# Flamingo block with gated cross attention on one core: the sums' turn and product a slot later, one output half in the next unit, weight and context transfers at two fixed places

## The chip, the cores and the metric

One core of a Trainium2 chip. The time is the device time of one execution in microseconds. Before the change it is 2407.74 us, the median of 3 runs (2406.89 to 2412.46). Engines are called by the profile's names: PE (TensorE), DVE (VectorE), ACT (ScalarE), POOL (GpSimd), SP or SyncE (which here only issues transfers).

## The reference, cut to what matters

```python
# x (4, 256, 512), ctx (4, 1601, 512); 32 heads of 128, 8 key/value heads
q = (layernorm(x) @ Wq + bq)                      # per head 256 x 128
k, v = split(ctx @ Wkv + bkv)
scores = einsum("blkgd,bmkd->bkglm", q, k) / sqrt(128)
o = einsum("bkglm,bmkd->blkgd", softmax(scores), v)
x = x + tanh(g_xattn) * (o @ Wo + bo)
x = x + tanh(g_ffn) * ffn(layernorm(x))           # base product and 2 of 8 LoRA experts
```

## The kernel before

The attention is cut into 64 **units**, U = 0 to 63: a batch b = U // 16 and two query heads (512 columns together). A unit has 13 **slots**, one for each tile t of up to 128 of the 1601 context rows. Every engine runs its own program over the same slots, s = 13 U + t, and all meet by semaphores. A slot of PE has always:

- the scores of tile s, three matmuls of 512 columns into `psS` (L414 to L416, each product is made of a high and a low part in fp32r),
- the value product of tile s - 20 (`VAL`), three matmuls into the unit's bank of `psW` (L611 to L613), from `ph` and `pl`,
- and the **jobs** that a table gives for this slot (`AT` and `AT_MEM`, lines 73 to 84, one row for each U % 4, one word for each slot). I call the units by U % 4 kind 0, 1, 2 and 3.

The jobs are: m, the turn of the running maximum of the unit before; s, the turn of the sums of the unit two before (four transposes of `psum_`, L470); r and b, the spreading of reciprocals and maxima over the rows by PE; q, k, v, the next projections; o0 and o1, the two halves of the output product of the unit two before, 6 matmuls of 512 columns each (`proj_o`, through L414 to L416); x, the turn of the next batch's rows.

Around a tile: ACT copies the scores to `xs` (L903), DVE takes the running maximum (`mrun`, L1271), POOL takes the maximum off (`xs`, L832, 17 slots behind), ACT makes the exponential twice, to `psP` (or `pp`, `psum_`) and to `ph` (L993, L996, 18 slots behind), DVE makes `pl` (L1057) and adds to `psum_` (L1302). From unit 16 on, tiles 0 to 2 of a unit are lowered by POOL (L836) and added there (`add_p`, L841), and POOL's `merge` (L847) adds its part to DVE's sums. The merge of one unit stands on POOL in front of the lowering of the next unit's tiles 0, 1 and 2: merge, take-off, lower 0, take-off, lower 1, take-off, lower 2.

For units 16 to 61 the maxima and for units 16 to 60 the sums go through memory (`max_by_mem`, `sum_by_mem`): DVE reduces the turned rows to 128 x 4 numbers, SyncE writes these to `scr_m` or `scr_r` (L690, L701), waits till they have landed, and reads them back as a 128 x 512 tile `mb` or `rbc` (L694, L705). POOL's first take-off of a unit needs `mb`. The sums' way is: s on PE (slot 5), DVE's reduce and reciprocal (L1220, L1222, slot 6), out and back on SyncE (placed at slot 6), DVE's product with `rbc` (L1279, in slot `on_slot`, 9), ACT's `oh` (L1028), DVE's `ol` (L1282, slot 10), o0 on PE (slot 11), o1 (slot 12). DVE works in order, so the product with `rbc` stands in front of the slot's `pl` and sums.

SyncE's program has one queue. Besides the two round trips it loads the weights of the next q, k, v and o (`load`, L673 and L674; 0.5 MB for q and k, 1 MB for v and o, high and low part together), the next batch's context in four pieces (`load_ctx`, L681 and L682, 1.5 MB each), and in units 19 to 26 and 35 to 42 it fetches, and later keeps, two cut pieces of the context of a later batch for each unit (`fetch` L641, `keep_ctx` L663 and L664; POOL cuts at slots 10 and 12, and `kept_at` puts the second keeping four slots later, into the next unit). A load stands in SyncE's program in the slot of the job that frees its place, and waits for that job. In units 18, 34 and 50 the accumulator `acc` is written to memory and the next one loaded (L764 to L770), with a wait for the first between them. SyncE isn't paced by slots, only by its waits.

## Time and profile before

| | |
|---|---|
| median of 3 runs | 2407.74 us |
| the profiled execution | 2417.14 us, its span 2415.2 us |
| busy: PE, weight loads, DVE, ACT, POOL | 2286.6, 1934.7, 1838.8, 1643.8, 1629.7 us |
| DMA packets, bytes | 148798, 282.14 MB |
| granted clock of PE, mean | 0.986 |

Busy time of PE includes matmuls that overlap, so its distance to the span is idle time, but busy time isn't all work. A stretch of the profile is given by its start and end in us from the span's start; I cut units at the first score matmul of their slot 0.

### The profile page before, as it was taken

What the parts mean: (1) busy time and instruction counts of PE and PEld (TensorE: products, weight loads), DVE (VectorE), ACT (ScalarE), POOL (GpSimd) and SP (SyncE); (2) the same over time, 40 slices, a digit from 0 to 9 for tenths busy, and PEclk for the clock granted to TensorE, in tenths of its full rate; (3) what the DMA queues carried; (4) which work ended last, traced back from release to release, by engine and by line L of the source; (5) the groups of instructions that cost most, each with busy time, mean ns of one, the idle gap of its engine ahead of it and who ended that gap; (6) DMA issues with size and microseconds to landing.
All of it is one profiled execution on the core that took longest, in us unless ns stands there. A gap on an engine that the chain in (4) does not pass through costs nothing.

```text
span 2415.2 us, 37259 instructions
## 1 busy us (share of the span) xinstructions
PE 2286.6 (95%) x12205; PEld 1934.7 (80%) x12205; DVE 1838.8 (76%) x3162; ACT 1643.8 (68%) x3117; POOL 1629.7 (67%) x1372
## 2 busy tenths in 40 slices
PE   7999999999999999898999999999899999999888
PEld 6888888888878788787888878788688887878765
DVE  5887988888776777777777767677678778678765
ACT  4776777777676676666777666676667767676653
POOL 5797887877477586675667676765756756656662
PEclk9999999999999999999999999999999999999999
DMA  7344433462234434345243244334433233233301
GB/s 255 128 154 132 133 128 119 155 229 97 100 91 123 119 117 134 92 130 175 62 130 115 83 139 124 114 104 130 146 87 109 85 102 89 65 114 84 92 36 53
DMA packets 148798, 282.14 MB, mean 117 GB/s; under 512 B 27904, under 2 KB 61184, under 8 KB 148352
## 3 DMA queue, kind: packets, MB, share of 16 engines
q1 hardware_dynamic: 148608, 279.77, 36.8%
q8 instruction: 99, 1.62, 0.3%
q14 instruction: 91, 0.75, 0.1%
HBM read 212.66 MB, written 67.05 MB: 116 GB/s over the span
## 4 chain that ended last, share of the span: by engine, by line
PE 76%; DVE 7%; POOL 5%; DMA 5%; issue 3%; ACT 3%; SPq 1%; DVEq 0%; POOLq 0%; ACTq 0%
PE psW L414 12%; PE psW L415 11%; PE psW L416 11%; PE psW L611 6%; PE psS L416 6%; PE psS L414 6%; PE psS L415 6%; PE psW L612 6%; PE psW L613 6%; PE psW L470 3%; DMA scr_r<-rinv 3%; POOL psum_ L847 2%; DVE mrun L1271 2%; DVE psum_ L1302 2%; POOL xs L832 2%
## 5 line engine op out<-in xcount | busy, mean ns | idle before, releaser
L832 POOL TENSOR_TENSOR xs<-xs,mb 128x512 f32<-128x512 f32 (+1 forms) x832 | 1066.3, 1308 | 431.5 <-DMA mb<-scr_m 387.9
L1271 DVE TENSOR_TENSOR mrun<-psS,mrun 128x512 f32<-128x512 f32 (+1 forms) x704 | 484.3, 688 | 416.0 <-ACT xs L903 414.9
L903 ACT ACTIVATE xs<-psS 128x512 f32<-128x512 f32 (+1 forms) x832 | 496.3, 597 | 280.7 <-PE psS L416 270.1
L996 ACT ACTIVATE ph<-xs 128x512 fp32r<-128x512 f32 (+1 forms) x832 | 520.1, 625 | 0.9 <-PE psW L613 0.9
L1057 DVE TENSOR_TENSOR pl<-psP,ph 128x512 fp32r<-128x512 f32 (+1 forms) x672 | 458.2, 682 | 27.9 <-ACT ph L996 25.0
L1302 DVE TENSOR_TENSOR psum_<-psP,psum_ 128x512 f32<-128x512 f32 (+1 forms) x672 | 456.2, 679 | 0.0
L993 ACT ACTIVATE psP<-xs 128x512 f32<-128x512 f32 (+1 forms) x672 | 402.1, 598 | 1.7 <-DVE psum_ L1302 1.6
L611 PE MATMUL psW<-ph,vh 128*128 128x512 f32 (+1 forms) x832 | 341.0, 410 | 44.2 <-DVE pl L1057 30.8
L414 PE MATMUL psS<-ql,kh 128*128 128x512 f32 (+1 forms) x832 | 339.2, 408 | 7.0 <-DVE mrun L1271 5.7
L612 PE MATMUL psW<-pl,vh 128*128 128x512 f32 (+1 forms) x832 | 330.1, 397 | 0.0
L613 PE MATMUL psW<-ph,vl 128*128 128x512 f32 (+1 forms) x832 | 330.1, 397 | 0.0
L415 PE MATMUL psS<-qh,kh 128*128 128x512 f32 (+1 forms) x832 | 329.4, 396 | 0.0
L416 PE MATMUL psS<-qh,kl 128*128 128x512 f32 (+1 forms) x832 | 329.3, 396 | 0.0
L611 PEld LDWEIGHTS psW<-ph,vh 128*128 128x128 f32 (+1 forms) x832 | 157.7, 189 | 109.2 <-DVE pl L1057 39.7
L414 PE MATMUL psW<-wvl,ch 128*128 128x256 f32 (+1 forms) x832 | 240.2, 289 | 4.4 <-DVE vl L1057 4.4
L415 PE MATMUL psW<-wvh,ch 128*128 128x256 f32 (+1 forms) x832 | 235.1, 283 | 0.0
L416 PE MATMUL psW<-wvh,cl 128*128 128x256 f32 (+1 forms) x832 | 234.5, 282 | 0.0
L613 PEld LDWEIGHTS psW<-ph,vl 128*128 128x128 f32 (+1 forms) x832 | 157.7, 190 | 38.3
L908 ACT ACTIVATE kh<-psW,bkv_sb 128x384 fp32r<-128x384 f32 (+1 forms) x128 | 76.4, 597 | 163.1 <-PE psW L416 163.1
L612 PEld LDWEIGHTS psW<-pl,vh 128*128 128x128 f32 (+1 forms) x832 | 158.5, 190 | 34.6 <-issue 1.7
L416 PEld LDWEIGHTS psS<-qh,kl 128*128 128x128 f32 (+1 forms) x832 | 153.9, 185 | 39.6 <-issue 1.0
L414 PE MATMUL psW<-cl,wkh 128*128 128x384 f32 (+1 forms) x512 | 177.7, 347 | 5.4 <-DVE cl L1057 5.4
(185 smaller groups left out, 4454.5 us busy)
## 6 DMA issues: line engine op xcount, KB each, us to landing
wqh<-scr_wq SPq DMA_DIRECT2D x96, 256.0 KB, 3.9
wql<-scr_wq SPq DMA_DIRECT2D x96, 256.0 KB, 4.4
woh<-scr_wo SPq DMA_DIRECT2D x48, 512.0 KB, 5.1
wol<-scr_wo SPq DMA_DIRECT2D x48, 512.0 KB, 6.9
mb<-scr_m SPq DMA_DIRECT2D x46, 256.0 KB, 4.2
rbc<-scr_r SPq DMA_DIRECT2D x45, 256.0 KB, 3.7
scr_wq<-wqh SPq DMA_DIRECT2D x32, 256.0 KB, 2.0
scr_wq<-wql SPq DMA_DIRECT2D x32, 256.0 KB, 2.5
```

The source lines that it names most:

```text
L414: eng.matmul(o, lh, rl, start=first, stop=False)
L415: eng.matmul(o, lh, rh, start=False, stop=False)
L416: return eng.matmul(o, ll, rh, start=False, stop=last)
L611: eng.matmul(o, vh[0:rows, t, hs], hi, start=t == 0, stop=False)
L612: eng.matmul(o, vh[0:rows, t, hs], lo, start=False, stop=False)
L613: eng.matmul(o, vl[0:rows, t, hs], hi, start=False, stop=t == NT - 1).then_inc(s_pv)
L832: eng.tensor_tensor(tile, tile, mb[0:rows_of(t), U % 2, :], ALU.subtract).then_inc(s_sub)
L903: return eng.activation(hi, src, ACT.Copy)
L996: eng.activation(ph[0:rows, T % RP, :], xs[0:rows, T % RX, :], ACT.Exp).then_inc(s_h)
L1057: return eng.tensor_tensor(lo, src, f32(hi), ALU.subtract)
L1271: eng.tensor_tensor(run, psS[0:rows, s % 2, :], a, ALU.max).then_inc(s_m)
L1302: eng.tensor_tensor(total, p, total, ALU.add).then_inc(s_a)
```

## The change

What it does, in units 18 to 61 (`quiet`, the units whose sums went through memory before, less the last):

- the sums' turn s stands in slot 6, the product with `rbc` in slot 10, `oh` in 10, `ol` in 11, o0 in slot 12, and o1 in slot 0 of the next unit, behind m. The other jobs are moved around them: in kind 0 there are v0 to v4 in slots 7 to 11, in kind 1 v7 is in slot 5 and slot 10 is empty, in kind 2 q0 and k3 stand a slot later and v11, v12 in slots 2 and 3; POOL's steps stay.
- SyncE places the sums' round trip at slot 7, and the transfers that stood beside the jobs at slot 3 (first q half, o) and slot 9 (second q half, k, v). The context pieces are loaded at slot 9 of a batch's unit 13, slots 3 and 9 of unit 14 and slot 3 of unit 15.
- POOL's second context cut of a unit stands in slot 11, and both pieces are kept a slot behind their cut, in the same unit.
- the accumulator's way out and in stands at slot 3 of units 18, 34, 50, behind the loads of that slot, and DVE's statistics at slot 2.
- the sums of unit 60 go through PE (`MEM_SUM` is one less), so unit 62 has the old table's job r and its o0 in slot 10.

```diff
-    MEM_LO, MEM_MAX, MEM_SUM = 16, UN - 2, UN - 3
+    MEM_LO, MEM_MAX, MEM_SUM = 16, UN - 2, UN - 4
...
+    def quiet(U):
+        return U >= 2 and sum_by_mem(U - 2)
...
     def on_slot(V):
-        return 9 if sum_by_mem(V) else 8
+        return 10 if sum_by_mem(V) else 8
...
     AT_MEM = [
-        "m q0 b k3 q1 s - v0 v1 v2 v3 o0 o1",
-        "m,v4 v5 b,q0 v6 k0 s,v7 q1 k1 v8 v9 v10 o0 o1",
-        "m,v11 k2 b,v12 q0 k3 s - - q1 - - o0,x0 o1,x1",
-        "m q0 b k0 q1 s k1 - - k2 - o0 o1",
+        "m q0 b k3 q1 - s v0 v1 v2 v3 v4 o0",
+        "m v5 b,q0 v6 k0 v7 s,q1 k1 v8 v9 - v10 o0",
+        "m k2 b,v11 v12 q0 k3 s - q1 - - x0 o0,x1",
+        "m q0 b k0 q1 - s,k1 - - k2 - - o0",
     ]
...
+        if U >= 3 and sum_by_mem(U - 3):
+            jobs[NT * U].append(("o", U - 3, 1))
...
-        cuts[NT * (NU * b + 3 + i // 2) + (10, 12)[i % 2]].append(("c", n, 0))
+        cuts[NT * (NU * b + 3 + i // 2) + (10, 11)[i % 2]].append(("c", n, 0))
...
-                if t == 6 and sum_by_mem(U - 2):
+                if t == 7 and quiet(U):
                     sum_to_lanes(U - 2)
...
-                for kind, n, part in jobs[s]:
+                for kind, n, part in [] if quiet(U) else jobs[s]:
...
+                if quiet(U) and t == 3 and 2 * U + 4 < 2 * UN:
+                    load("q", 2 * U + 4, 2 * NU, s_q, 2 * U + 3)
+                if t == 3 and U >= 3 and sum_by_mem(U - 3):
+                    load("o", U - 2, NU, s_o, 2 * U - 4)
+                if quiet(U) and t == 9:
+                    if 2 * U + 5 < 2 * UN:
+                        load("q", 2 * U + 5, 2 * NU, s_q, 2 * U + 4)
+                    if U % 2 == 0 and U // 2 + 1 < NK:
+                        load("k", U // 2 + 1, 8, s_k, 2 * U + 4)
+                    if U % 4 == 2 and U // 4 + 1 < 4 * B:
+                        load("v", U // 4 + 1, 4, s_v, NT * (U // 4) + NT)
+                if quiet(U) and b + 1 < B and (u, t) in ((13, 9), (14, 3), (14, 9), (15, 3)):
+                    load_ctx(b + 1, ((13, 9), (14, 3), (14, 9), (15, 3)).index((u, t)))
...
-                if u == 2 and t == 1 and 1 <= b < B:
+                if u == 2 and t == 3 and 1 <= b < B:
                     sp.wait_ge(s_acd, 32 * b)
```

PE in unit 44 (kind 0), from the value product of slot 5 on. `psum_` is the sums' tile, `psS` the scores of the next slot. Before:

```order
L611 MATMUL psW<-ph,vh 128x512
L612 MATMUL psW<-pl,vh 128x512
L613 MATMUL psW<-ph,vl 128x512
L470 MATMUL psW<-ident,psum_ 128x128 x4
L414 MATMUL psS<-ql,kh 128x512
L415 MATMUL psS<-qh,kh 128x512
L416 MATMUL psS<-qh,kl 128x512
L611 MATMUL psW<-ph,vh 128x512
L612 MATMUL psW<-pl,vh 128x512
L613 MATMUL psW<-ph,vl 128x512
L414 MATMUL psS<-ql,kh 128x512
```

and with the change:

```order
L614 MATMUL psW<-ph,vh 128x512
L615 MATMUL psW<-pl,vh 128x512
L616 MATMUL psW<-ph,vl 128x512
L417 MATMUL psS<-ql,kh 128x512
L418 MATMUL psS<-qh,kh 128x512
L419 MATMUL psS<-qh,kl 128x512
L614 MATMUL psW<-ph,vh 128x512
L615 MATMUL psW<-pl,vh 128x512
L616 MATMUL psW<-ph,vl 128x512
L473 MATMUL psW<-ident,psum_ 128x128 x4
L417 MATMUL psS<-ql,kh 128x512
```

The turn of the sums stands one whole slot (six matmuls) further on, with nothing put in front of it in this kind.

SyncE in unit 22, from behind the maxima's way back up to the reciprocals' way out (`scr_c` and `stg` are the context pieces, `wv`, `wq`, `wo`, `wk` the weights, h and l their high and low parts). Before:

```order
L673 DMA wvh<-scr_wv 128x1024
L674 DMA wvl<-scr_wv 128x1024
L663 DMA scr_c<-cst 128x384
L664 DMA scr_c<-stg 128x384
L641 DMA stg<-in_ctxT 128x384
L673 DMA wqh<-scr_wq 128x512
L674 DMA wql<-scr_wq 128x512
L673 DMA woh<-scr_wo 128x1024
L674 DMA wol<-scr_wo 128x1024
L673 DMA wkh<-scr_wk 128x512
L674 DMA wkl<-scr_wk 128x512
L701 DMA scr_r<-rinv 128x4
```

and with the change:

```order
L644 DMA stg<-in_ctxT 128x384
L676 DMA wqh<-scr_wq 128x512
L677 DMA wql<-scr_wq 128x512
L676 DMA woh<-scr_wo 128x1024
L677 DMA wol<-scr_wo 128x1024
L704 DMA scr_r<-rinv 128x4
```

Four weight transfers are left in front of the reciprocals where there were eight, and the keeping of a context piece is gone from here.

SyncE in the same unit, from behind the reciprocals' way back to the maxima of the unit after (`scr_m`). Before:

```order
L673 DMA wqh<-scr_wq 128x512
L674 DMA wql<-scr_wq 128x512
L663 DMA scr_c<-cst 128x384
L664 DMA scr_c<-stg 128x384
L641 DMA stg<-in_ctxT 128x384
L690 DMA scr_m<-nm 128x4
```

and with the change:

```order
L676 DMA wqh<-scr_wq 128x512
L677 DMA wql<-scr_wq 128x512
L676 DMA wkh<-scr_wk 128x512
L677 DMA wkl<-scr_wk 128x512
L676 DMA wvh<-scr_wv 128x1024
L677 DMA wvl<-scr_wv 128x1024
L666 DMA scr_c<-cst 128x384
L667 DMA scr_c<-stg 128x384
L666 DMA scr_c<-cst 128x384
L667 DMA scr_c<-stg 128x384
L644 DMA stg<-in_ctxT 128x384
L693 DMA scr_m<-nm 128x4
```

The weights of k and v and both context pieces now stand here, in front of the maxima.

## Rows read from the trace of the kernel before

**Rows 1.** The page: the chain that ended last, by line; transfers, median us to landing.
```profile
PE psW L414 12%; PE psW L415 11%; PE psW L416 11%; PE psW L611 6%; PE psS L416 6%; PE psS L414 6%; PE psS L415 6%; PE psW L612 6%; PE psW L613 6%; PE psW L470 3%; DMA scr_r<-rinv 3%; POOL psum_ L847 2%; DVE mrun L1271 2%; DVE psum_ L1302 2%; POOL xs L832 2%
...
rbc<-scr_r SPq DMA_DIRECT2D x45, 256.0 KB, 3.7
```

**Rows 2.** PE's groups by form: busy us, mean ns, idle before, releasers.
```profile
L611 PE MATMUL psW<-ph,vh 128*128 128x512 f32 x768 | 315.1, 410 | 44.2 <-DVE pl L1057 30.8 <-POOL pl L836 13.4
...
L414 PE MATMUL psW<-wol,oh 128*128 128x512 f32 x256 | 106.6, 416 | 16.9 <-issue 15.3 <-POOL wkh L820 1.1 <-DVE ol L1282 0.5
...
L470 PE MATMUL psW<-ident,psum_ 128*128 128x128 f32 x256 | 45.7, 301 | 30.0 <-POOL psum_ L847 28.3 <-DVE psum_ L1307 1.7
```

**Rows 3.** Stretches of one unit each: 44, 45, 50, 43, 57, 62; us, then busy us of PE, PEld, DVE, ACT, POOL, clock, DMA share, GB/s.
```profile
1603.81:1637.89 34.08, 33.06 (x184) 28.36 (x182) 27.21 (x47) 24.64 (x47) 23.45 (x19) 1.00 0.34 94
1637.89:1677.25 39.36, 39.13 (x232) 34.68 (x230) 28.67 (x51) 26.55 (x51) 22.98 (x19) 1.00 0.46 148
1827.21:1862.08 34.87, 32.95 (x171) 27.32 (x170) 28.45 (x50) 24.46 (x46) 21.15 (x17) 1.00 0.47 151
1570.34:1603.81 33.47, 31.78 (x160) 26.70 (x158) 25.48 (x44) 23.99 (x45) 21.98 (x18) 1.00 0.32 93
2071.51:2114.61 43.10, 40.67 (x232) 36.18 (x230) 29.27 (x57) 28.87 (x54) 22.91 (x19) 0.96 0.22 62
2256.44:2301.12 44.68, 37.46 (x175) 30.25 (x174) 35.25 (x49) 25.05 (x47) 22.12 (x17) 0.89 0.35 106
```

**Rows 4.** The same for units 22, 36 and 46.
```profile
791.25:832.75 41.50, 35.70 (x171) 29.17 (x170) 27.82 (x48) 24.45 (x46) 26.66 (x23) 0.92 0.43 131
1305.04:1340.97 35.93, 33.39 (x183) 28.21 (x182) 26.99 (x47) 24.63 (x47) 28.18 (x25) 1.00 0.43 125
1677.25:1720.17 42.92, 35.41 (x180) 28.93 (x178) 27.62 (x48) 25.04 (x47) 26.76 (x20) 0.92 0.55 190
```

**Rows 5.** Timeline of unit 44, slots 4 to 7: start, us, engine, idle before.
```profile
1613.23 2.56 POOL L832 TENSOR_TENSOR xs<-xs,mb 128x512 f32<-128x512 f32 x2 [8.62 <-DMA mb<-scr_m]
...
1617.80 1.27 POOL L847 TENSOR_TENSOR psum_<-pp,psum_ 128x512 f32<-128x512 f32 x1 [2.01 <-DVE psum_ L1302]
...
1619.13 0.75 PE L470 MATMUL psW<-ident,psum_ 128*128 128x128 f32 x4 [1.02 <-POOL psum_ L847]
...
1620.27 1.30 POOL L836 TENSOR_TENSOR pl<-psum_,ph 128x512 fp32r<-128x512 f32 x1
...
1621.80 0.40 PE L611 MATMUL psW<-ph,vh 128*128 128x512 f32 x1
```

**Rows 6.** Timeline of unit 22, slots 6 to 11, SyncE's queue, DVE and PE.
```profile
811.13 1.49 SPq L701 DMA_DIRECT2D scr_r<-rinv  x1
...
818.18 0.32 SPq L705 DMA_DIRECT2D rbc<-scr_r  x1
...
822.19 0.70 DVE L1279 TENSOR_TENSOR psW<-psW,rbc 128x512 f32<-128x512 f32 x1 [3.78 <-DMA rbc<-scr_r]
...
823.92 0.50 PE L611 MATMUL psW<-ph,vh 128*128 128x512 f32 x1 [4.08 <-DVE pl L1057]
```

**Rows 7.** Instructions and transfers of scr_r: the 45 ways out of the reciprocals.
```profile
DMA to landing us min/median/max: 1.4/3.4/9.6
```

**Rows 8.** SyncE's timeline, unit 34: the accumulator out and in.
```profile
1241.19 0.42 SPq L764 DMA_DIRECT2D scr_x<-acc  x1
1246.12 0.32 SPq L767 DMA_DIRECT2D acc<-scr_b  x1
```

**Rows 9.** Timeline of unit 62, slots 9 to 11.
```profile
2281.50 7.80 DVE L1131 TENSOR_SCALAR hn<-x,mv,rstd 128x512 f32<-128x512 f32 x1
...
2284.08 4.93 POOL L832 TENSOR_TENSOR xs<-xs,mb 128x512 f32<-128x512 f32 x4
...
2290.05 0.76 PE L414 MATMUL psS<-ql,kh 128*128 128x512 f32 x1 [5.73 <-DVE mrun L1271]
```

**Rows 10.** Timeline of unit 57, slot 5: the turn of the sums.
```profile
2090.72 0.85 PE L470 MATMUL psW<-ident,psum_ 128*128 128x128 f32 x4 [2.43 <-POOL psum_ L847]
```

More of the change, by code:

```diff
@@ L86, in gated_block @@
         names_of = {0: "k1 - k2 v0 q0 k3 q1 v1 - v2 - v3 -", UN: "- - - - - s - r - - o0 - o1",
-                    UN + 1: "- - - - - s - r - - o0 o1"}.get(U, (AT_MEM if U >= 2 and sum_by_mem(U - 2) else AT)[U % 4])
+                    UN + 1: "- - - - - s - r - - o0 o1"}.get(U, (AT_MEM if quiet(U) else AT)[U % 4])
         for t, names in enumerate(names_of.split()):
@@ L134, in gated_block @@
         b, i = divmod(n, 16)
-        cuts[NT * (NU * b + 3 + i // 2) + (10, 12)[i % 2]].append(("c", n, 0))
+        cuts[NT * (NU * b + 3 + i // 2) + (10, 11)[i % 2]].append(("c", n, 0))
     cut_at = [(p, 0) for p in first] + [(p, s) for s in range(SLOTS) for p in cuts[s]]
     order = [p for p, s in cut_at]
-    def kept_at(z):
-        return z + 4 if z > NT * NU and z % NT == 12 else z + 1
     fetches = {s: [] for s in range(SLOTS)}
@@ L152, in gated_block @@
         if no >= len(first) + 2:
-            s = max(s, at - 10, kept_at(cut_at[last][1]))
+            s = max(s, at - 10, cut_at[last][1] + 1)
             assert s <= at, (p, at, s)
@@ L734, in _ @@
                     max_to_lanes(U - 1)
-                if t == 6 and sum_by_mem(U - 2):
+                if t == 7 and quiet(U):
                     sum_to_lanes(U - 2)
-                for kind, n, part in [p for z in (s - 4, s - 1) if kept_at(z) == s for p in cuts.get(z, [])]:
+                for kind, n, part in cuts.get(s - 1, []):
                     if kind == "c":
@@ L754, in _ @@
                         load_ctx(n // 8 + 1, part)
-                if t == 3 and sum_by_mem(U - 3):
-                    load("o", U - 2, NU, s_o, 2 * (U - 3) + 2)
-                if u == 14 and t == 1 and b + 1 < B:
+                if quiet(U) and t == 3 and 2 * U + 4 < 2 * UN:
[11 more added lines that the diff above has]
+                    load_ctx(b + 1, ((13, 9), (14, 3), (14, 9), (15, 3)).index((u, t)))
+                if (u, t) == ((13, 11) if b else (14, 1)) and b + 1 < B:
                     sp.wait_ge(s_xt, 2 * b + 2)
@@ L1324, in _ @@
                     dve.wait_ge(s_stat, 1)
-                if u == 2 and t == 0 and 1 <= b < B:
+                if u == 2 and t == 2 and 1 <= b < B:
                     for i in range(2):
```

## The prediction

> **What bounds the kernel now.** I read the page's chain first: it runs through PE's matmuls, and its largest piece that isn't compute is the way of the reciprocals to memory, 3% of the span [rows 1]. PE is busy for 2286.6 of 2415.2 us, so all its gaps together are 129 us. Next come PE's groups by form, for what ends the gaps [rows 2]: value products wait 44.2 us, 30.8 of it for `pl` by DVE and 13.4 for `pl` by POOL; the turn of the sums waits 30.0 us, 28.3 of it for POOL's merge; o0 waits 16.9 us. These three are 91 us, and the change touches each.
>
> Then the units themselves. An ordinary unit of kind 0, 1, 2, 3 takes 34.08, 39.36, 34.87 and 33.47 us [rows 3]. Some take more: 22 and 46, both kind 2, take 41.50 and 42.92, and 36, kind 0, takes 35.93 [rows 4]. Six units of kind 2 are like the first two (22, 26, 30, 38, 42, 46), three of kind 0 like the third (20, 36, 40). Units 57 and 62 stand out for reasons of their own, 43.10 and 44.68 us [rows 3].
>
> The timeline of unit 22 shows why: the reciprocals' way out is issued at 811.13, but the way back only at 818.18, 7.05 us later, since it waits for the 2 KB to land. DVE waits 3.78 us at the product with `rbc` and, working in order, reaches `pl` late; PE stands 4.08 us at the value product behind it [rows 6]. In front of these 2 KB SyncE has just issued the eight weight transfers, after a context piece had held it up. Over all 45 the way out takes 1.4 us at the least, 3.4 as median and 9.6 at most [rows 7], the last in a unit where a piece of the next batch's context stands in front.
>
> **The change, part by part.**
>
> *Late reciprocals.* Unit 22 is 6.6 us over an ordinary kind 2, 46 is 8.1 over. I take 6.6 for each of six, 39.6 us; for the three of kind 0, whose worst is 1.85 over, 1.5 each, 4.5 us. With the change the k and v weights and the kept pieces stand behind the round trip, so this goes: **44.1 us**. Two things stay in front.
>
> In units 30 and 46, q, o and a context piece (3 MB) are issued when q0 ends in slot 4. I count from there. A slot is six matmuls of 512 columns; in unit 44 nine of these and the four transposes take 2.67 us [rows 5], so 0.235 each, 1.4 us for a slot, 0.5 for a turn, and a k3 about 2.4. The turn ends at 3.8 + 1.9 = 5.7 us, the reciprocals are ready at 6.7, and DVE comes to the product in slot 10 at about 13.3 (slots 7 to 9 with q1, 5.6, then scores, copy and maximum of slot 10, 2.0). The longest way out landed after 9.6 us [rows 7], with such a piece issued just before it; here the piece has 4 us of start, so I take 4 to 8 us. The way back takes 3.7 [rows 1]: `rbc` is there at 14.4 to 18.4, 1 to 5 us late. As a third of the bytes that stood there are gone, I take 1.5 for each: **-3.0 us**.
>
> In units 18, 34 and 50 the accumulator's way out stands behind q and o, and SyncE waits for it: 4.93 us when it had only `mb` in front of it [rows 8]. Issued at 2 us and landed at 7 to 10, it holds the reciprocals' way out by 0 to 3 us, of which a margin of 1 to 2 us is free. I take 1 each: **-3.0 us**.
>
> The Trainium skill (DMA: Bandwidth & Descriptors, Queues, rings and completion order) says that a transfer's semaphore increment lands only after every earlier write of the same DMA engine. By it position in SyncE's program decides, as rows 6 and 7 also look, and it speaks against the change in these five units alone, where large transfers are moved ahead of the small one.
>
> *The slots.* The turn's cover is one slot. But POOL's chain behind the merge isn't moved. In unit 44 [rows 5] POOL's merge runs 1617.80 to 1619.07, the turn waits for it, POOL's lowering of tile 0 runs 1620.27 to 1621.57, and PE takes tile 0's value product at 1621.80. With the change PE does slot 6 first, comes to the turn at about 1619.4 without a wait, and is at the value product of slot 7 at 1620.6, where it now waits till 1621.6. So **kind 0** gains 0.2 us, not the 1.2 that the turn's wait seems to give: the lowering is late next. **Kind 1** has v7 and q1 there as well, 2.8 us more of cover; its share of the turn's wait goes, 0.7. **Kind 2** has k3 (2.4 us) in front of the turn, so its waits for the turn (0.3) and for POOL's lowering (1.1; with kind 3 these are the 13.4 us of rows 2) go. Its o0 wait stays: DVE has product, lowering and sums of two slots to do while PE has empty slots, before and after. Less a bit for DVE's queue, 1.0. **Kind 3** keeps slots 7 and 8 empty, so POOL's lowering of tile 2 stays late, and the product in slot 10 no longer has k2 (2.1 us) beside it: its o0 wait grows by about a microsecond, which eats the 0.5 to 0.7 gained before. I take -0.3. The sum is 1.6 us in four units; units 18 to 61 are eleven of each kind: **17.6 us**. The ends: nothing or -5 if DVE's queue is worse, and 40 if half of all idle time in the four (7.8 us) goes.
>
> o1 in slot 0 adds 1.4 us of PE work there and takes it from slot 12: nothing. It gives POOL's chain more room: in unit 44 the first take-offs wait for `mb` till 1613.23, end at 1615.79, and POOL then is idle 2.01 us till the merge can start [rows 5]. With o1 this margin becomes 3.4.
>
> *Unit 57* is 3.7 us over its kind [rows 3]. ACT's detour for the statistics makes the merge late, and the turn waits 2.43 us for it [rows 10]. With v7 and a slot of scores and values, 2.8 us, in front, all of it goes: **3.0 us** beside the 0.7 counted above; bounds 0 and 3.0.
>
> *Unit 62* is 9.8 us over its kind. It loses the round trip. But DVE's normalisation `hn` takes 7.80 us here and PE waits 5.73 us for the maximum behind it [rows 9]; `rbc` is not what it waits for, and `hn` stays where it is. I take only a share of what follows it, as `ol` is one slot earlier: **2.5 us**; bounds 0 and 9.8.
>
> The Trainium skill (SBUF — State Buffer, Who interferes with whom) states that DVE in a two-port mode and GpSimd exclude each other for whole instructions. The timeline agrees: `hn` ends 2289.30, just behind POOL's row of take-offs, 2289.01 [rows 9]. If instead the round trip were the cause, this term would be 9.8 and the sum 7 us more.
>
> *The rest.* The spread of unit 60's reciprocals by PE is 0.5 us, once. Loads at slot 9 have over half a unit till their use: nothing.
>
> **Sum.** 44.1 - 3.0 - 3.0 + 17.6 + 3.0 + 2.5 - 0.5 = 60.7 us. The profiled execution took 2417.1, so it would show 2356.4; it lies 9.4 over the median of the runs, which stands for 2407.7 - 60.7 = **2347 us**.
>
> **The rivals.**
>
> *The slots bring nothing or cost.* If the waits only move, from the turn to POOL's lowering and from slot 11 to slot 12, in all four kinds, the slots' term is -5 to 5, and the five crowded units may stand at their upper ends (another 10 us off): 2365 to 2382. For it speaks kind 0, where I count just this; against it that kinds 1 and 2 have work to put there. Chance 0.22.
>
> *The slots bring all.* If o0's waits go too, which would need DVE's queue to be shorter than I read it, the term is 40 and unit 62 may give more: 2307 to 2327. Against it is that slots 9 to 11 are empty in kind 2. Chance 0.12.
>
> *The maxima become late instead.* Context pieces and k and v weights now stand before the maxima's way out, which `mb` and POOL's first take-off wait for. The margin is 2.0 + 1.4 us in kinds 0 and 3 and more in the others. If the way out took 7 us, as the reciprocals' did [rows 6], `mb` would be 5.6 later; 22 units at 2.2 us and nothing in the others are 48 us, and with POOL's whole chain late in all 44 units by over 2 us it is past the gain: 2347 + 88 = 2435, slower. It decides from a delay of 3.4 us, and is slower than before from about 5 us in kinds 0 and 3 and the other two hit as well. Against it: these loads are issued a third of a unit before the maxima, and only 16 units have context pieces. Chance 0.04.
>
> *The change doesn't reach the reciprocals:* SyncE comes to its slot 7 no sooner than before, as q0's load is still waited for in kind 2. Then only the slots count, 2385 to 2400. But q0 ends 6 us before they are ready. Chance 0.04.
>
> **How the numbers follow.** My forecast's own case, 2330 to 2364, has 0.58. With the two next to it the range 2322 to 2382 leaves out about 2 in 10. A measurement of this kernel can tell 0.3% (7 us) from no change: faster 0.94, within it 0.02, slower 0.04.
>
> **What would show it.** In the profile after: the waits for `rbc` by DVE's product near zero but in units 18, 30, 34, 46, 50; unit 22 at 34 us; the turn's wait for POOL under 3 us in all, with a wait of the value product for POOL's lowering that grows from 13.4 to 20 us or more; o0 waiting longer in kind 3; unit 57 near 39 us; unit 62 above 41. Wrong would be: kind 0 shorter by over a microsecond, take-offs waiting for `mb` until the merge is due, or unit 62 at 35 us.

## The result and the profile after

| | before | after |
|---|---|---|
| median of 4 runs each | 2408.64 us (2406.89 to 2412.46) | 2389.33 us (2385.76 to 2395.64) |
| the profiled execution, its span | 2417.14, 2415.2 us | 2395.64, 2393.7 us |
| granted clock of PE, mean | 0.986 | 0.988 |

After to before is 0.9921, with a 95% interval of 0.9896 to 0.9945: some 19 us faster, where 61 were forecast. The direction is right, and the time lies above the range. One execution among all runs, the profiled one of the first run below, took 4477.52 us; it counts in the median of that run alone, and the kernel was run once more for its trace.

PE's groups by form, after: busy us, mean ns, idle before, releasers; to be read beside [rows 2].

```profile
L614 PE MATMUL psW<-ph,vh 128*128 128x512 f32 x768 | 317.6, 413 | 48.0 <-DVE pl L1072 25.9 <-POOL pl L851 21.6
...
L417 PE MATMUL psW<-wol,oh 128*128 128x512 f32 x256 | 110.6, 432 | 31.3 <-issue 29.7 <-POOL wkh L835 1.1 <-DVE ol L1297 0.5
...
L473 PE MATMUL psW<-ident,psum_ 128*128 128x128 f32 x256 | 40.2, 279 | 3.3 <-DVE psum_ L1322 1.7 <-POOL psum_ L862 1.6
```

The turn's wait is gone, 30.0 to 3.3 us, and the other two have grown: the value products wait 8.2 us more for POOL's `pl`, though 4.9 less for DVE's, and o0 waits 14.4 us more. The three were 91.1 us and are 82.6. Not all of the o0 row's growth is the slots': unit 62 has 5.6 us of the 14.4, since its wait of 5.73 us stood at the scores before [rows 9] and stands at o0 now, 6.33 us (the line is shown further down). Units of kind 3 have 6.1 us of it and those of kind 2 have 2.7.

Units of the changed kernel, in this order 44, 45, 54, 43 (ordinary, kinds 0 to 3), then 22, 30, 34, 50, 57 and 62; columns as in [rows 3].

```profile
1581.85:1617.41 35.56, 34.49 (x195) 29.90 (x194) 27.67 (x49) 25.05 (x48) 23.63 (x19) 1.00 0.27 90
1617.41:1655.08 37.67, 37.67 (x220) 33.34 (x219) 27.59 (x48) 26.07 (x50) 22.85 (x19) 1.00 0.40 126
1952.35:1986.82 34.47, 32.91 (x172) 27.43 (x170) 27.12 (x47) 24.45 (x46) 20.43 (x17) 1.00 0.41 123
1547.71:1581.85 34.14, 32.03 (x159) 26.63 (x158) 26.36 (x45) 24.07 (x45) 28.50 (x24) 1.00 0.32 96
790.18:824.65 34.47, 32.91 (x172) 27.42 (x171) 27.10 (x47) 24.44 (x46) 23.00 (x19) 1.00 0.49 150
1073.88:1113.30 39.42, 35.80 (x180) 29.74 (x178) 29.17 (x51) 24.93 (x47) 25.39 (x19) 0.93 0.53 166
1221.21:1262.75 41.54, 34.98 (x171) 28.71 (x170) 29.75 (x53) 24.44 (x46) 22.52 (x18) 0.90 0.47 132
1803.98:1844.98 41.00, 34.82 (x172) 28.58 (x171) 29.57 (x53) 24.45 (x46) 22.53 (x18) 0.92 0.43 128
2056.51:2094.28 37.77, 37.77 (x219) 33.14 (x218) 28.10 (x54) 28.49 (x53) 22.22 (x18) 1.00 0.22 71
2236.11:2279.23 43.12, 36.63 (x185) 30.26 (x184) 35.37 (x51) 25.22 (x48) 21.24 (x17) 0.92 0.33 104
```

Three readings come straight from these lengths.

- Unit 22 is an ordinary unit now, and so are 26, 38 and 42, and 20, 36 and 40: of the 29.1 us that these seven were over their kind, 28.6 are gone.
- The four kinds take 34.08 + 39.36 + 34.87 + 33.47 = 141.78 us before [rows 3] and 35.56 + 37.67 + 34.47 + 34.14 = 141.84 after. A v (1.4 us) went from kind 1 to kind 0; beyond that nothing was gained in four units.
- Units 34 and 50, ordinary before (50 was 34.87 [rows 3]), take 41.54 and 41.00. Unit 30 takes 39.42 and unit 46 40.22. The four are 24.3 us over their kind, and the units behind them (31, 35, 47) another 2.6. In units 30 and 46 some 0.8 us each is no wait but the turns of the next batch's rows, which the others of their kind don't have (an estimate from the kernel before: unit 14, which has them, takes 34.79 us and unit 10, which hasn't, 34.02).

The timelines of unit 34 show the third: SyncE's queue from the first load of slot 3 on, with the end of DVE's reciprocals between, then DVE's and PE's late instruction.

```profile
1236.63 0.32 SPq L676 DMA_DIRECT2D wqh<-scr_wq  x1
...
1238.41 0.43 SPq L779 DMA_DIRECT2D scr_x<-acc  x1
...
1243.72 0.18 DVE L1237 RECIPROCAL rinv<-ssum 128x4 f32<-128x4 f32 x1
...
1247.37 0.32 SPq L782 DMA_DIRECT2D acc<-scr_b  x1
1247.79 0.38 SPq L704 DMA_DIRECT2D scr_r<-rinv  x1
1251.61 0.32 SPq L708 DMA_DIRECT2D rbc<-scr_r  x1
...
1256.66 0.70 DVE L1294 TENSOR_TENSOR psW<-psW,rbc 128x512 f32<-128x512 f32 x1 [5.46 <-DMA rbc<-scr_r]
...
1258.00 0.79 PE L614 MATMUL psW<-ph,vh 128*128 128x512 f32 x1 [5.78 <-DVE pl L1072]
```

SyncE stands 8.96 us between the accumulator's way out and its way in, and the reciprocals' way out is behind both: ready at 1243.90, it is issued 3.9 us later. It then takes 3.82 us, and DVE's product starts when the way back has landed, 5.05 after its issue. This is the same row of waits as in unit 22 before [rows 6], with other bytes in front. The way out is slow here (1.44 us in the ordinary unit 54), the way back isn't: its median over the kernel is

```profile
rbc<-scr_r SPq DMA_DIRECT2D x44, 256.0 KB, 4.5
```

where it was 3.7 [rows 1], and in unit 54 it takes 5.3, so that DVE's product there starts only 0.2 us after it has landed. SyncE issues 2 MB of weights 1.3 us behind it (slot 9); whether they slow it no run separates. Behind PE's 5.78 us of standing, the rest of the slot runs at another clock; the window from there to the unit's end (its seventh number is the granted clock) is

```profile
1258.00:1262.75 4.75, 4.34 (x9) 3.00 (x10) 4.70 (x8) 3.12 (x7) 0.11 (x1) 0.50 0.74 292
```

0.50 is 1.2 GHz, where it had been 1.00, 2.4 GHz, ahead of the wait. PE is busy for 34.98 us in unit 34 and for 32.91 in its like, unit 54, so the fallen clock adds some 2 us to the wait.

The second reading first in kind 0. POOL and PE of unit 44, to be read beside [rows 5]:

```profile
1597.24 1.30 POOL L862 TENSOR_TENSOR psum_<-pp,psum_ 128x512 f32<-128x512 f32 x1 [3.35 <-DVE psum_ L1317]
1598.49 1.31 POOL L847 TENSOR_TENSOR xs<-xs,mb 128x512 f32<-128x512 f32 x1
...
1598.78 0.63 PE L473 MATMUL psW<-ident,psum_ 128*128 128x128 f32 x4
...
1599.75 1.28 POOL L851 TENSOR_TENSOR pl<-psum_,ph 128x512 fp32r<-128x512 f32 x1
...
1601.18 0.47 PE L614 MATMUL psW<-ph,vh 128*128 128x512 f32 x1 [1.07 <-POOL pl L851]
```

The turn doesn't wait, as forecast, and the value product two steps on waits for the lowering, as forecast. POOL is idle for 3.35 us ahead of the merge (3.4 forecast), and only then, behind the merge, makes the take-off that stands in front of the lowering.

In kinds 2 and 3 the o0 wait is the one to look at. Before, in units 50 and 43:

```profile
1857.88 0.47 PE L414 MATMUL psW<-wol,oh 128*128 128x512 f32 x1 [0.94 <-issue]
1599.61 0.47 PE L414 MATMUL psW<-wol,oh 128*128 128x512 f32 x1 [0.39 <-issue]
```

and after, in units 54, 43 and 62:

```profile
1985.37 0.47 PE L417 MATMUL psW<-wol,oh 128*128 128x512 f32 x1 [1.08 <-issue]
1580.40 0.47 PE L417 MATMUL psW<-wol,oh 128*128 128x512 f32 x1 [0.94 <-issue]
2271.76 0.76 PE L417 MATMUL psW<-wol,oh 128*128 128x512 f32 x1 [6.33 <-issue]
```

Kind 2 had this wait before as well; it is kind 3 where it grew, by 0.55 us. What else the four kinds gained and gave back per unit: kind 0 lost its turn's wait of 1.02 us and got 1.07 at the lowering; kind 1 lost 0.23 at the turn; kind 2 lost 0.80 at the lowering and got 0.26 at the scores, for DVE's maximum, and 0.14 at o0; kind 3 lost 0.98 at the turn and got 0.50 more at the lowering, 0.34 for DVE's `pl` and the 0.55 at o0.

### The profile page after: what moved, and what is told of

It reads as the page before. It is cut to its first block, busy times and chain, and to the rows that moved or that the text cites. A ratio compares the mean times of both kernels' runs of the same rounds, so it can differ in the third digit from the quotient of the medians.

```text
span 2393.7 us, 37301 instructions
## 1 busy us (share of the span) xinstructions
PE 2281.9 (95%) x12209; PEld 1935.1 (81%) x12209; DVE 1838.1 (77%) x3162; ACT 1643.9 (69%) x3118; POOL 1627.5 (68%) x1372
## 4 chain that ended last, share of the span: by engine, by line
PE 76%; POOL 9%; DVE 6%; issue 3%; DMA 3%; ACT 2%; SPq 0%; POOLq 0%; ACTq 0%; DVEq 0%
PE psW L417 12%; PE psW L418 11%; PE psW L419 11%; PE psW L614 7%; PE psW L616 6%; PE psS L419 6%; PE psW L615 6%; PE psS L417 6%; PE psS L418 6%; POOL xs L847 4%; POOL pl L851 3%; PE psW L473 2%; DVE pl L1072 2%; POOL psum_ L862 1%; ACT xs L918 1%
## 5 line engine op out<-in xcount | busy, mean ns | idle before, releaser
L862 POOL TENSOR_TENSOR psum_<-pp,psum_ 128x512 f32<-128x512 f32 x47 | 60.9, 1295 | 191.5 <-DVE psum_ L1317 191.5
```

## The experiments

Each is the changed kernel with the edit shown; times are medians, and all ratios are to the kernel before, run on the same chip. The kernel before gave 2410.55, 2410.68 and 2413.76 us in the three sets. The changed kernel ran only beside the 2408.64 us above, so a distance to it or from one set to another carries 2 to 5 us of which chip it was.

**The accumulator ahead of the o load.**

```diff
-                if u == 2 and t == 3 and 1 <= b < B:
+                if u == 2 and t == 2 and 1 <= b < B:
                     sp.wait_ge(s_acd, 32 * b)
```

> The changed kernel, with the accumulator's way out and in placed at slot 2 of units 18, 34 and 50, before the loads of slot 3, instead of behind them. Nothing else differs. Theory A (transfers that the change left in front of the reciprocals' way out hold it up, through SyncE's wait for the accumulator): units 34 and 50, which took 41.54 and 41.00 us in the changed kernel, fall to 34.5 like the other units of kind 2, and the time falls by 12 to 14 us, to about 2376. Theory B (the wait is in DVE's statistics or the accumulator's sum itself, not in the queue): both units stay at 41 us and the time at 2389.

> The kernel of e1_acc_early once more, for its trace. By theory A of that run (the o load ahead of the accumulator's way out and in is what made it late) the accumulator is out and in before the trip of the reciprocals: units 34 and 50 within 1.5 us of their kind (34.5 us) instead of 41.5 and 41.0, acc in at least 3 us earlier against the unit's start; the rest of the kernel unchanged, one time of 2374 to 2380 us.

Measured: 2377.65 us, 0.9866 [0.9846, 0.9887], 11.7 below the changed kernel (2376.86 us without the execution of 4477.52 us); one more, for the trace, took 2379.01. That is in the 2374 to 2380 of theory A. In that trace unit 50 takes 34.80 us, and unit 34 is this:

```profile
1218.58:1253.31 34.73, 33.06 (x171) 27.43 (x170) 28.41 (x51) 24.44 (x46) 20.37 (x17) 1.00 0.49 158
```

and SyncE's queue in unit 34, with DVE's last statistics between:

```profile
1224.74 0.32 SPq L779 DMA_DIRECT2D scr_x<-acc  x1
...
1230.15 0.69 DVE L1116 BATCH_NORM_STATS2 steps<-acc 128x6 f32<-128x512 f32 x1
...
1230.92 0.32 SPq L782 DMA_DIRECT2D acc<-scr_b  x1
1233.99 0.32 SPq L676 DMA_DIRECT2D wqh<-scr_wq  x1
...
1241.29 0.32 SPq L704 DMA_DIRECT2D scr_r<-rinv  x1
1242.73 0.32 SPq L708 DMA_DIRECT2D rbc<-scr_r  x1
```

The accumulator is on its way 6.2 us after the unit's start instead of 17.2, since SyncE doesn't stand at the q load's wait for the job of slot 4 first. The way in is still issued 6.18 us after the way out, but that is no longer the transfer: the way out has landed after 3.8 us (8.9 in the changed kernel), and the way in also waits for DVE's statistics of `acc`, whose sums end at 1230.84. It is on its way before q and o are issued, and the reciprocals are out 1.44 us after their issue. One slot in SyncE's program is 13 us in the two units, and theory A holds with its size.

**Context pieces apart from the round trip.**

```diff
-                if quiet(U) and b + 1 < B and (u, t) in ((13, 9), (14, 3), (14, 9), (15, 3)):
-                    load_ctx(b + 1, ((13, 9), (14, 3), (14, 9), (15, 3)).index((u, t)))
+                for c in {(13, 9): (0, 1), (14, 9): (2,), (15, 3): (3,)}.get((u, t), ()):
+                    if quiet(U) and b + 1 < B:
+                        load_ctx(b + 1, c)
```

> The changed kernel, with the second context piece loaded together with the first, at slot 9 of a batch's unit 13, instead of at slot 3 of unit 14. Theory A (bytes in front of the 2 KB decide): unit 30 falls from 39.42 to 34.5 and unit 46 from 40.22 to 34.5, the units behind them (31 and 47, 34.68 and 35.46) stay 0.5 to 1.3 over their kind, since the third piece still stands in front of the maxima; together -10 to -11 us, to about 2379. Theory B (the 3 MB only move: now the maxima of unit 29, which stand behind q and two pieces, come late, and POOL with them): unit 30 keeps 2 us or more, as a wait of POOL for mb beyond the merge, and the gain is under 6 us.

Measured: 2387.26 us, 0.9909 [0.9892, 0.9926], 2 below the changed kernel. Units 30 and 46 came down to 37.61 and 37.63, not to 34.5. With the piece gone from in front of the trip, PE's turn of the next batch's second x tile (`cst`) was late in both, by 2.6 us, behind DVE's `xtl` of the first. The time is as theory B had it, but its reason is not: no product waits for `rbc` in these two units any more, and PE's wait is not POOL's for `mb`. Nor could they come to 34.5, since their x turns alone are some 0.8 us. My first explanation was that the x loads, at slot 11 of units 29 and 45 (the change moved them there from slot 1 of units 30 and 46, which the list of what it does leaves out), stood behind 3 MB of context. Two later runs, with the x loads ahead of the context and with POOL's normalizations elsewhere, test it.

**POOL's take-off ahead of its merge.**

```diff
-                "S0,S1 M,S2 L0,S3 L1,S4 L2,S5 A2,S6 S7 S8 S9 S10 S11 S12 -",
+                "S0,S1,S2 M L0,S3 L1,S4 L2,S5 A2,S6 S7 S8 S9 S10 S11 S12 -",
```

> The changed kernel, with POOL's take-off of tile 2 in front of its merge instead of behind it; the order of all else stays. Theory A (what holds PE in kinds 0 and 3 is POOL's chain behind the merge: merge, take-off, lower 0, take-off, lower 1, take-off, lower 2): POOL is idle 3.35 us in front of the merge, so the take-off costs nothing there, and the lowering comes 1.3 us sooner. Kind 0 loses its wait at slot 7 (1.40 us), kind 3 0.5 to 1.1 at slot 9, kind 2 nothing: -20 to -25 us, to about 2367. Theory B (the wait would only move on, to o0 at slot 12 behind DVE's queue): kind 0, with v0 to v4 in front of o0, still gains, kind 3 nothing: -10 to -15 us. Theory C (ACT's exponential of tile 0 is late, not POOL): no change, 2389.

Measured: 2376.13 us, 0.986 [0.9842, 0.9878], 13 below. Units 44 and 43 of its trace:

```profile
1571.20:1605.63 34.43, 34.43 (x196) 29.91 (x194) 27.66 (x49) 25.04 (x48) 23.75 (x19) 1.00 0.33 93
1537.78:1571.20 33.42, 31.84 (x159) 26.71 (x158) 26.39 (x45) 23.98 (x45) 28.66 (x24) 1.00 0.29 94
```

Kind 0 is 1.13 us shorter and kind 3 0.72, so eleven of each would be 20 us. Some of it is given back: in kind 3 units of the stretches with context cuts (unit 39 takes 34.91) the turn in slot 6 waits again for POOL. The time is in theory B's range, while kind 3 does gain, as theory A had it.

**The old slots.** Before's table of jobs, product at slot 9, round trip at slot 6; transfers, cuts and the rest as changed.

```diff
-        return 10 if sum_by_mem(V) else 8
+        return 9 if sum_by_mem(V) else 8
...
-                if t == 7 and quiet(U):
+                if t == 6 and quiet(U):
```

> The changed kernel with the slots of before: the job table with the turn in slot 5, the product in slot 9, o0 and o1 in slots 11 and 12 of one unit, the round trip at slot 6. SyncE's two places, the context pieces, the accumulator at slot 3 and unit 62 through PE stay. Theory A (the slots bring nothing but in unit 57): as the changed kernel plus the 3.6 us of unit 57, so 2391 to 2395; kinds 0 to 3 at 34.08, 39.36, 34.9 and 33.5 us as before the change, and the turn waits for POOL again. The forecast's theory (the slots bring 17.6 us besides): 2410. In kind 2 there is now less time between slot 3's transfers and the reciprocals' way out than with the new slots by nothing (q0 is a slot earlier as well), so units 30, 34, 46, 50 stay long.

Measured: 2396.67 us, 0.994 [0.9917, 0.9964], 7.3 over the changed kernel, with intervals of the ratios that overlap; 1.7 above theory A's range and 13 below what the forecast's 17.6 us would make. Units 44, 45, 54, 43 and 57:

```profile
1583.94:1618.03 34.09, 33.06 (x184) 28.38 (x183) 27.18 (x47) 24.67 (x47) 23.40 (x19) 1.00 0.34 94
1618.03:1657.41 39.38, 39.14 (x232) 34.68 (x231) 28.67 (x51) 26.59 (x51) 22.93 (x19) 1.00 0.41 121
1953.41:1988.31 34.90, 32.96 (x171) 27.31 (x170) 26.88 (x46) 24.47 (x46) 21.15 (x17) 1.00 0.40 121
1550.43:1583.94 33.51, 31.83 (x159) 26.72 (x158) 26.03 (x45) 23.90 (x45) 28.81 (x24) 1.00 0.32 93
2055.90:2099.28 43.38, 40.69 (x232) 36.08 (x230) 29.28 (x57) 28.89 (x54) 22.74 (x19) 0.96 0.22 61
```

The first four are 141.88 us, before's lengths one by one and the changed kernel's sum: the slots alone bring nothing in ordinary units. Units 22, 26, 38 and 42 are at 34.90 to 34.93 here and 20, 36 and 40 at 34.09, so the late reciprocals went by the transfers' places and not by the slots. Unit 57 is long again, 4.0 us over its kind. That is about what the slots brought: the two profiled executions have spans of 2396.3 and 2393.7 us; the rest of the 7.3 between the medians is within the spread.

**`ol` a slot earlier,** behind `pl` and the running sum of the product's own slot.

```diff
-                if 0 <= V < UN and t == on_slot(V) + 1:
-                    dve.wait_ge(s_oh, V + 1)
-                    eng.scalar_tensor_tensor(ol[:, :], bank_of(("pv", V, 0)), ...
...
+                if 0 <= V < UN and t == on_slot(V):
+                    dve.wait_ge(s_oh, V + 1)
+                    eng.scalar_tensor_tensor(ol[:, :], bank_of(("pv", V, 0)), ...
```

> The changed kernel, with one DVE instruction elsewhere: ol, the lower part of the turned output, is formed at the end of slot 10 behind pl and the running sum, instead of in slot 11 behind the running maximum. In the changed kernel's trace o0 in slot 12 waits for it in units with U % 4 = 2 and 3 (issue 1.08 us in unit 54, 0.94 us in unit 43), where slot 12 loses 1.8 us; the kinds 0 and 1 have an empty slot or little wait there. Theory A (what the slots saved at the turn came back as this wait): some 0.9 us off in two of four units, 11 groups of four, so 15 to 20 us, 2369 to 2375 us beside 2389. Theory B (the wait only hands on to the running maximum and the next scores, since DVE stands at ol until ACT has oh): within 4 us of the changed kernel, with slot 12 shorter and slot 11 or the next slot 0 longer by as much.

Measured: 2368.76 us, 0.9819 [0.9803, 0.9834], 20.6 below the changed kernel. The output product's wait in its groups by form:

```profile
L417 PE MATMUL psW<-wol,oh 128*128 128x512 f32 x256 | 107.9, 422 | 7.4 <-issue 7.4
```

It falls from 31.3 to 7.4 us, of which 8.2 are unit 62's and come back there as a wait of 6.25 us at the scores. Ordinary units of kinds 2 and 3 take 33.71 and 33.56 instead of 34.47 and 34.14, and kind 1 37.47 instead of 37.66. The gain has theory A's size, a little over. But it isn't only what the slots had moved: kind 2, which gains most, waited 0.94 us for o0 in the kernel before too. No run has this edit with the old slots, so how much of the 20.6 us needs the new ones isn't shown. In the changed kernel the wait is DVE's queue: in unit 54 the product, `pl`, the sums and the maximum of slot 11 follow each other without a gap, and `ol` comes last.

```profile
1981.98 0.69 DVE L1294 TENSOR_TENSOR psW<-psW,rbc 128x512 f32<-128x512 f32 x1
1982.58 0.68 DVE L1072 TENSOR_TENSOR pl<-psP,ph 128x512 fp32r<-128x512 f32 x1
1983.18 0.68 DVE L1317 TENSOR_TENSOR psum_<-psP,psum_ 128x512 f32<-128x512 f32 x1
1983.91 0.69 DVE L1286 TENSOR_TENSOR mrun<-psS,mrun 128x512 f32<-128x512 f32 x1
1984.52 0.74 DVE L1297 SCALAR_TENSOR_TENSOR ol<-psW,bkv_sb,oh 128x512 fp32r<-128x512 f32 x1
```

PE's o0 starts at 1985.37, 0.11 behind the end of `ol`. The profile puts PE's 1.08 us down to "issue"; the run shows that it was `ol`.

**Three edits together.** The accumulator at slot 2, the take-off first, the context pieces apart, each as above, and the x loads ahead of the context:

```diff
-                if (u, t) == ((13, 11) if b else (14, 1)) and b + 1 < B:
+                if (u, t) == ((13, 8) if b else (14, 1)) and b + 1 < B:
```

> The changed kernel with three edits: accumulator out and in at slot 2 of its unit, GpSimd's take-off of slot 2 ahead of the merge, context pieces 0 and 1 at slot 9 of unit 13, 2 and 3 at slots 9 and 3 of the next two units, and the next x loads at slot 8 of unit 13, ahead of the context. Theory A (the losses lie in different units, so the gains add): 12 for the accumulator, 13 for the take-off, 2 for the pieces and 2 x 4.5 for the x loads that stood behind the context in that experiment, together 36, so 2350 to 2358 us, and units 30 and 46 within 1 us of their kind (34.5), units 34 and 50 within 3. Theory B (the pieces only choose which transfer is late): units 30 and 46 keep over 2 us, 2360 to 2366.

Measured: 2357.58 us, 0.9776 [0.9761, 0.9791]. One by one the three had brought 27 us, together they bring 31.8: the gains add, and nothing shows where the rest comes from. Units 34 and 50 are at 34.45 and 34.58. But units 30 and 46 still take 37.61 and 37.63, exactly what they took with the x loads behind the context. So the x loads' place was not it, and my explanation falls, though the time is at the edge of theory A's range.

**The same with `ol` in slot 10,** by the edit shown above.

> The three edits together and ol at the end of slot 10. Theory A: what ol brings alone comes off here too, since it lies in another slot (12) of the units than the take-off's (7 and 9): e6_three_together minus e5's gain, 2336 to 2342 if e5 gives 15 to 20. Theory B: nothing beyond e6_three_together.

Measured: 2341.11 us, 0.9709 [0.9691, 0.9727], 16.5 below the last. The two edits meet no common limit. Unit 30 is at 37.63 once more; POOL there, while PE is in slots 9 to 12, makes two normalizations between its take-offs:

```profile
1084.37 2.07 POOL L902 TENSOR_SCALAR xraw<-xraw,mv,rstds 128x512 f32<-128x512 f32 x1
1086.43 2.07 POOL L902 TENSOR_SCALAR cst<-cst,mv,rstds 128x512 f32<-128x512 f32 x1
```

**The old slots with the take-off first,** the two edits above together.

> The kernel with the old slots of jobs (before's table, product at slot 9, turn of the sums at slots 4 and 5, reciprocals' trip at slot 6), the rest as changed (2396.7 us when it ran), and with GpSimd's take-off of slot 2 ahead of the merge. It tells whether the 13 us of the take-off are the new slots' gain set free or GpSimd's order alone. Theory A (the new slots leave the turn time for the merge, and only so can the take-off go first): with the turn in slot 5 again, the merge 1 us later makes it wait 1 us longer, and units come out as without the edit or longer, 2395 to 2408 us. Theory B (GpSimd's order was the only limit): 2380 to 2386 us.

Measured: 2398.45 us, 0.9947 [0.9932, 0.9962], the old slots' time within the spread. PE's turn of the sums in it:

```profile
L470 PE MATMUL psW<-ident,psum_ 128*128 128x128 f32 x256 | 45.8, 303 | 37.2 <-POOL psum_ L859 35.4 <-DVE psum_ L1319 1.7
```

The turn waits 37.2 us here, 32.9 with the old slots alone, 30.0 in the kernel before [rows 2]. Theory A has the time, but its reason only in part: in an ordinary unit of kind 0 the turn waits 1.02 us as before and not a microsecond more, because the take-off fits into POOL's idle time and PE waits for the merge, which comes no sooner. Units 23, 27 and 39 are 8.7 us longer together than with the old slots alone. (Unit 62 happens to be 8.8 us shorter, of which more at the end; without that the edit would have cost.) The same edit brings 13 us with the new slots and nothing or less with the old ones: only where PE no longer waits for the merge does it matter what stands behind the merge. The new slots' worth is thus room that POOL's order did not use.

**GpSimd's normalizations of x at another place.** The kernel of the three edits and `ol`, with

```diff
-                if u == 14 and t == 8 and b + 1 < B:
+                if u == 14 and t == (3 if b else 8) and b + 1 < B:
                     pool.wait_ge(s_stat, 1)
```

> The kernel of e7_together_ol with GpSimd's two normalizations of the next x tiles (x_norm, 2.07 us each, one behind the other) at slot 3 of units 30 and 46, where GpSimd waits for its maxima, instead of slot 8. In e7_together_ol units 30 and 46 lose 4.74 and 4.77 us in slot 12, their kind elsewhere 1.08. Theory A (not a transfer but GpSimd: the 4.1 us of the two stand ahead of its add and of the take-offs, so ACT's exponentials, DVE's queue and the bank of the first x turn are late): 3.7 off in each of the two units, 7.4 in all, 2332 to 2336 beside 2341. Theory B (PE's turn waits for the x tiles' transfer or for its bank whatever GpSimd does): within 2 us of 2341.

Measured: 2340.37 us, 0.9694 [0.9669, 0.9718]; by the medians nothing. In the trace units 30 and 46 fell to 35.88 and 35.86, 1.8 us each, half of what A expected. The median doesn't resolve 3.5 us here: five runs lie between 2333.70 and 2343.22, and other units (27 with 36.90 for 34.01) were longer in this trace.

**The context as changed.** The last kernel, with the pieces and the x loads where the change has them.

> e9_x_norm_early with the context pieces and the x loads where the changed kernel has them (pieces at slot 9 of unit 13, 3 and 9 of 14, 3 of 15; x loads at slot 11 of unit 13, for units 29 and 45). It tells how much of the 5 us that units 30 and 46 lost beyond their kind in the changed kernel is transfers ahead of the reciprocals' trip and how much GpSimd's normalizations. Theory A (mostly GpSimd): within 3 us of e9. Theory B (mostly the piece at slot 3, 1.5 MB ahead of the trip at slot 7): units 30 and 46 lose 3 to 5 us each in slot 12, 6 to 10 us beyond e9.

Measured: 2345.22 us, 0.9719 [0.9694, 0.9743], 4.9 over the last. Units 30 and 46 take 39.29 and 38.93, 6.5 us more together, at the lower end of theory B, whose 6 to 10 us of time the median doesn't reach. So with the normalizations out of the way the transfers ahead of the trip cost 3.4 and 3.1 us in these units, and with the transfers out of the way the normalizations cost 1.8. The two waits hide each other: moving the transfers alone had given 1.8 and 2.6 us in the changed kernel, and unit 30 with only the normalizations moved (39.29) is hardly shorter than with neither (39.45 in the run of `ol` alone). With both moved, units 30 and 46 are still 2.1 us over the 33.8 of their kind, of which some 0.8 is the x turns; PE waits 1.4 us for DVE's `xtl` at the second of them. What makes that late is open.

**`hn` on GpSimd.** The kernel of the normalizations' run, with the first `hn` of unit 62 on the other engine.

```diff
-                if s in (TN - 14, TN - 11):
-                    i = 2 if s == TN - 14 else 4
+                if s in (TN - 17, TN - 14, TN - 11):
+                    i = {TN - 17: 0, TN - 14: 2, TN - 11: 4}[s]
...
-                for i in {TN - 18: (0,), TN - 17: (1,), ...
+                for i in {TN - 17: (1,), ...
```

> e9_x_norm_early with the first ffn normalization of unit 62 (hn, TENSOR_SCALAR, 5.99 us on DVE in e7_together_ol, 7.24 in the changed kernel, 1.05 in e8_old_slots_takeoff) moved from DVE to GpSimd, at slot 9 behind its add. Theory A (on DVE it waits until GpSimd's unbroken run of work ends, 2270.1 in the changed kernel's trace, and does not work for that long; on GpSimd it costs its own 2.07 us): slot 10 of unit 62 loses 2 us instead of 4.5 and slot 11 under 1 instead of 1.5, together 3 to 4 us off, 2328 to 2333. Theory B (GpSimd's take-offs are what unit 62 waits for, hn only stands beside them): no gain, or up to 2 us more.

Measured: 2331.67 us, 0.9662 [0.9639, 0.9685], 8.7 below it. Unit 62 takes 35.72 us, after 42.11; GpSimd's `hn` takes 2.07 us there, and this is the unit:

```profile
2181.95:2217.67 35.72, 35.20 (x185) 29.21 (x184) 28.33 (x49) 25.48 (x48) 20.59 (x16) 1.00 0.41 126
```

Theory A holds, and in the unit's length with nearly twice its size. This is the fastest of the kernels: 3.4% below the kernel before, and 58 us below the changed kernel.

## Why the prediction was right and wrong

*What bounds the kernel* was read rightly: the reciprocals' trip, the turn, the value products and o0 are what the runs could move. POOL's normalizations of x it does not have.

*Late reciprocals, 44.1 us.* In the seven units where nothing large stands in front, 28.6 us went for the 30.9 of the forecast; over all nine the units were 44.4 over their kind. The rule of the Trainium skill that the prediction weighed (DMA: Bandwidth & Descriptors, Queues, rings and completion order) agrees with the traces of this case: 7.05 us for 2 KB behind transfers [rows 6], 1.44 us in unit 34 once the accumulator is ahead. Of the five units that it pointed at, four were late.

*The crowded units, 6.0 us: this term failed first, they cost 26.9.* For unit 34 I took the accumulator's way out to land 7 to 10 us after the loads' issue; it did at 10.7. The reciprocals were ready 7.3 us after it (6.7 by my count), so they were held 3.9 us and not "0 to 3". And I let their way out behind it run at its undisturbed 1.4 us; it took 3.8, issued right behind 0.5 MB of `acc` coming in. These two add in a row, 6.3 us. Against them stood no "margin of 1 to 2 us": I had taken 3.7 us for the way back, and in this kernel it takes up to 5.3 with nothing in front, which leaves 0.2 us to spare in unit 54. Unit 34's took 5.0, 0.3 less, and DVE came to the product about half a microsecond after `rbc` would have been there; that leaves the 5.46 us which the row shows. With the fallen clock it makes 7.1 and 6.5 us in units 34 and 50 against "1 each". Unit 18, with no o load in front, takes 33.34 us; it has 1.4 us less to do than its kind (no o1 of an earlier unit), so it lost about 0.3. For units 30 and 46 the forecast of `rbc` "1 to 5 us late" was right, DVE waited 2.9 and 3.7 us. Then I took 1.5 "as a third of the bytes that stood there are gone", which no row said: the lateness went to PE whole, as 3.2 and 4.0 us at the value product, and the clock in the 5.4 us behind it was 0.50 in unit 30. That POOL's two normalizations of x would be the next wait once the transfers are away I had not seen at all.

*The slots, 17.6 us: the second term that failed, they gave nothing.* This was the first rival, chance 0.22, and its 2365 to 2382 was still too low, since it left the crowded units at 16 us. By kinds: in kind 0 I had +0.2, it was -0.1 (1.48 longer, with a v of 1.4 moved in). Kind 1 had +0.7, was +0.3. Kind 2 had +1.0, was +0.4. Kind 3 had -0.3, was -0.7. Part of it I had read wrongly off the kernel before: a unit of kind 1 waits 0.23 us for the turn and not 0.7, one of kind 2 doesn't wait for the turn at all (I had 0.3), and for the lowering 0.80 and not 1.1. That is 1.1 us in four units that weren't there to be gained. "Its o0 wait stays" was right for kind 2, 0.94 and 1.08 us. Kind 3's o0 wait grew by 0.55, for which I had "about a microsecond". What I left out is what comes back elsewhere: 0.26 us at the scores in kind 2 ("less a bit for DVE's queue"), 0.34 at DVE's `pl` and 0.50 more at POOL's lowering in kind 3, and in kind 0 the lowering took all of the turn's wait and not all but 0.2 us. The upper end of 40 had no ground either: all idle time of PE in the four units is 4.9 us by [rows 3], 141.78 less 136.92 busy, so that half of it is 27 us in eleven groups and not 40.

*Unit 57, 3.0:* measured 3.74 over its kind before, 0.10 after, so 3.6. *Unit 62, 2.5:* 1.6, although it took in 1.4 us of work that I hadn't counted, o1 of unit 59. That `hn` and not `rbc` is what it waits for was right, and the last run shows it: the wait went with `hn`, to a unit of 35.72 us. The second rule that was weighed (SBUF — State Buffer, Who interferes with whom) agrees with this trace as with the one before, where `hn` on DVE ends with POOL's row of work; one other run, at the end, has it otherwise. The rows are these, DVE and POOL of unit 62 of the changed kernel:

```profile
2263.16 7.24 DVE L1146 TENSOR_SCALAR hn<-x,mv,rstd 128x512 f32<-128x512 f32 x1
...
2265.20 4.92 POOL L847 TENSOR_TENSOR xs<-xs,mb 128x512 f32<-128x512 f32 x4
```

POOL ends at 2270.12, `hn` at 2270.40.

**The sum again,** with what was measured in the profiled executions: 44.4 - 26.9 - 0.7 (eleven groups of four) + 3.6 + 1.6 is 22.0 us; unit 18 is 1.2 shorter beyond what its kind is, the units before it and the last stretch together 1.8 longer. That gives 21.4, and the two profiled executions are 21.5 us apart, the medians 19.3. Against the 60.7 of the forecast, the crowded units are 21 us short and the slots 18.

The maxima were never late (POOL is idle 3.35 us ahead of its merge), and SyncE came to the trip in time but in units 34 and 50, so the two small rivals were rightly small.

## What to carry to other kernels

A wait that goes away by shifting a chain is worth only what the next instruction of the same chain doesn't take back. Follow every engine's queue on to the next instruction that PE needs, and ask which engine's order must change too. Here the shift was worth nothing in ordinary units alone, and 13 us more came with one take-off moved, which did nothing without the shift. Moving `ol` gave 21 us with the shift; whether it needs it isn't shown. And when a small transfer with a late consumer is cleared in most places, cost the few that stay crowded by the sum in series, hold plus slowed way out, and take the margin against it from the kernel as it will be, not as it was: the way back's median had gone from 3.7 to 4.5 us. A position in an unpaced queue is the time of the last wait in front of it, not its slot.

## What was unexpected of the hardware

- The same DVE instruction, a TENSOR_SCALAR of 128x512 from SBUF to SBUF, took 7.24 us in the changed kernel, 5.99 in the kernel of the three edits and `ol`, and 1.05 in the one with the old slots and the take-off first:

```profile
2271.39 1.05 DVE L1143 TENSOR_SCALAR hn<-x,mv,rstd 128x512 f32<-128x512 f32 x1
```

  Each time it ran beside an unbroken row of POOL's work. Where it took 1.05 us, POOL's next instruction took 1.49 us instead of 1.28, and unit 62 was 34.19 us long. No row tells why it got in between POOL's instructions there and not elsewhere; that stays open.
- The accumulator's way out (0.5 MB) landed after 8.9 us with 1.5 MB issued just in front, and after 3.8 us with only `mb` in front. The way of 2 KB out varied from 1.4 to 9.6 us [rows 7] by what was issued ahead of it.
- With the take-off first, units 23, 27, 39 and 43 (kind 3, in or next to the stretches with context cuts) are 0.3 to 4.3 us over their kind in one trace or another, where the turn in slot 6 waits for POOL's merge, and not the same ones in each execution. No run separated the causes.
